# The global keys of a windowed attention: diagonal keys, and exponentials as the stationary operand

## What is computed

```
Q, K, V = x @ Wq.T + bq, x @ Wk.T + bk, x @ Wv.T + bv      # 16 heads of 8
s_loc  = Q . K over positions l-32 .. l+32, invalid ones masked
local  = softmax(s_loc) @ V_window
Kg, Vg = K[:, global_indices], V[:, global_indices]        # 25 global keys
glob   = softmax(Q . Kg * scale) @ Vg
out    = (0.7 * local + 0.3 * glob) @ Wo.T + bo
```

## Time and profile before

| | us |
|---|---|
| median of three runs | 1113.35 (1111.93 to 1116.1) |
| the profiled execution | 1111.69 |
| its span, first to last instruction | 1109.9 |
| TensorE busy | 961.9 (87%) |
| VectorE busy | 784.3 (71%) |
| GpSimd busy | 681.8 (61%) |
| ScalarE busy | 578.1 (52%) |

### The profile page before, as it was taken

How to read it: one execution, slowest core, us unless ns; L and a number is a source line. 1 busy time by engine, 2 the same in 40 slices (tenths; PEclk the granted TensorE clock), 3 DMA queues, 4 the chain that set the end, 5 groups by cost and what they waited for, 6 DMA issues and landing times.

```text
span 1109.9 us, 27990 instructions
## 1 busy us (share of the span) xinstructions
PE 961.9 (87%) x7664; PEld 709.4 (64%) x7664; DVE 784.3 (71%) x3615; ACT 578.1 (52%) x1250; POOL 681.8 (61%) x1491
## 2 busy tenths in 40 slices
PE   2999999999959995899999999999999419999950
PEld 1777777777734552677777777777776317877730
DVE  3788888888826786457776878777776327888845
ACT  2466676666621432255555555555555107777734
POOL 3566666666631222266768787888878623777765
PEclk9899999999978998599999999999999659999985
DMA  6121211111032442121112121222111157777717
GB/s 182 27 52 27 49 40 35 45 30 45 23 133 88 170 152 86 29 49 28 47 29 59 38 59 37 60 55 59 52 40 36 43 177 226 240 252 245 234 56 212
DMA packets 71376, 98.36 MB, mean 89 GB/s; under 512 B 13688, under 2 KB 43256, under 8 KB 71104
## 3 DMA queue, kind: packets, MB, share of 16 engines
q1 hardware_dynamic: 61040, 83.31, 25.6%
q0 software_dynamic: 4992, 10.30, 2.7%
q10 hardware_dynamic: 5232, 3.42, 1.2%
HBM read 49.48 MB, written 24.77 MB: 67 GB/s over the span
## 4 chain that ended last, share of the span: by engine, by line
PE 74%; DVE 9%; issue 6%; SPq 3%; DMA 3%; POOL 2%; ACT 2%; DVEq 0%; ACTq 0%; POOLq 0%
PE bank L348 6%; PE bank L172 5%; PE bank L253 4%; PE bank L357 4%; PE bank L378 4%; PE bank L1499 4%; PE bank L1500 4%; PE bank L1501 4%; PE bank L1265 4%; PE bank L412 4%; PE bank L419 3%; PE bank L168 3%; PE bank L352 3%; PE bank L387 3%; PE bank L404 2%
## 5 line engine op out<-in xcount | busy, mean ns | idle before, releaser
L536 ACT ACTIVATE p<-bank 128x480 f32<-128x480 f32 (+1 forms) x448 | 240.4, 540 | 256.3 <-PE bank L378 101.0
L671 DVE CUSTOM_DVE_ANT_0 bank<-bank,band 128x160 f32<-128x160 f32 x512 | 157.1, 348 | 80.7 <-PE bank L348 67.9
L671 DVE CUSTOM_DVE_ANT_0 bank<-bank,causal 128x128 f32<-128x128 f32 (+1 forms) x512 | 169.8, 388 | 56.4 <-PE bank L352 40.6
L901 POOL TENSOR_SCALAR_AFFINE_SELECT p<-p 128x380 f32<-128x380 f32 (+1 forms) x256 | 146.6, 602 | 63.2 <-ACT p L536 62.3
L1677 POOL DMA_INDIRECT y_rows<-p,rows x92 | 108.3, 1177 | 64.0 <-DVE p L1630 42.7
L671 DVE DVE_READ_ACCUMULATOR2_ANT nm<- 128x1 f32 x1024 | 145.5, 142 | 0.1
L882 POOL TENSOR_SCALAR_AFFINE_SELECT p<-p 128x256 f32<-128x256 f32 (+1 forms) x192 | 91.1, 486 | 69.1 <-ACT p L536 64.2
L348 PE MATMUL bank<-ks,qs 128*128 128x186 f32 x512 | 116.2, 311 | 3.1 <-issue 1.6
L348 PEld LDWEIGHTS bank<-ks,qs 128*128 128x128 f32 x512 | 79.6, 196 | 35.9 <-issue 21.0
L378 PE MATMUL bank<-qs,ks 128*128 128x160 f32 x512 | 100.4, 299 | 0.0
L1570 ACT ACTIVATE p<-bank,wb 128x512 f32<-128x512 f32 x92 | 63.6, 691 | 39.4 <-PE bank L1501 24.3
(11 more groups left out here) (209 smaller groups left out, 2369.0 us busy)
## 6 DMA issues: line engine op xcount, KB each, us to landing
qs<-parts SPq DMA_DIRECT2D x46, 512.0 KB
qs<-qf SPq DMA_DIRECT2D x128, 128.0 KB, 2.4
rows<-xr SPq DMA_DIRECT2D x23, 260.0 KB
parts<-ks SPq DMA_DIRECT2D x8, 512.0 KB
xs<-x_b SPq DMA_DIRECT2D x16, 256.0 KB
p<-in_w SPq DMA_DIRECT2D x12, 256.0 KB
xin<-in_x SPq DMA_DIRECT2D x16, 128.0 KB, 2.2
parts<-qf SPq DMA_DIRECT2D x4, 512.0 KB
```

Of the source, the lines that this page charges most:

```text
L536: act.activation(pb[:, :, :].rearrange("p u c -> p (u c)")[:, lo:lo + cols], bank[:, 0:cols], ACT.Exp, scale=SCALE).then_inc(L.exp_done, 1)
L671: return dve.tensor_tensor_reduce(at, at, mask, -1.0, -BIG, ALU.add, ALU.min, nm[:, item:item + 1])
L901: pool.affine_select(out=at, in_=at, compare_op=ALU.is_ge, fill=0.0, base=base, pattern=[[0, 4], [sign, hi - lo]], channel_multiplier=-sig ...
```

## The change

For the global keys of the second attention:

- `T.kg` becomes 128 columns wide for each t, with the keys of head group j in rows 32j and columns 32j of a block diagonal. One product of this with all 128 rows of the queries gives the scores of four heads, so pass 2 has its unit u = 3 only in j = 2 and 3, with two products of 256 columns each, in fp32r. They take the queries of all j from `T.qf`, of which there are now three, and which gets the rows of the maxima by four more transfers on SP's queue. `keep_kg` writes the diagonal with four `tensor_scalar` of 32 rows instead of one of 128, after pass 2 of (3,3), and counts `kg_kept` twice, once after the two copies and once at the end.
- ScalarE has two exponentials of 512 columns into `T.pg` instead of four of 256. Part 2 of `pv` is gone. In its place `global_values`, in (0,0) of the next iteration behind `round_pj(0)`, has the exponentials as the stationary operand and 64 columns of `vgb` moving, eight products, and leaves queries by channels in `T.og`. So `round_og` and the copy to `ogs` are gone, and `mx0` now stands behind `pj0` in its bank.
- `keep_vg` has one instruction instead of four.
- `round_kg` moves ahead, into (3,3) behind pass 1, and `keep_kg` behind the maxima of (3,3), ahead of `chosen` and `both_choices`. The identity products are gone.
- The new buffers lie in the room where the last layer holds its rows. Semaphore values are adapted; `unit2` numbers the units of pass 2. GpSimd clears the wider `kg` once at the start.

```
+        return 3 + 14 * (i - 1) + (0, 3, 6, 10)[j] + (u if j < 3 or i < B else u - 3)
...
+        if local and u == 3:
+            return self.late and j > 1
+        return self.pass2[j] and u < 3
...
-ROUNDS = (("pj0", "og", "mx0", "ont", "mx1", "y", "q1", "xt", "mx3"),
+ROUNDS = (("pj0", "mx0", "ont", "mx1", "y", "q1", "xt", "mx3"),
...
-        def round_og():
-            bank_read("og", i, p, th)
-            pe.wait_ge(L.ov_kept, L.kept * fin + 2)
+        def global_values():
+
+            pe.wait_ge(L.exp_done, L.unit2(i - 1, 3, 3) + 1)
+            pe.wait_ge(L.vg_kept, fin + 1)
+            wait(pe, L.on_done, fin)
             for tau in range(2):
-                for r in range(2):
-                    m = turn(T.mi[0][:, (2 * tau + r) * P:(2 * tau + r + 1) * P],
-                             T.ogs[:, r, tau * P:(tau + 1) * P])
-            m.then_inc(L.ot_done, 1)
+                out = T.og[:, tau * S:(tau + 1) * S].rearrange("p (r t z) -> p r t z", r=2, t=4)
+                for t in range(4):
+                    m = pe.matmul(out[:, :, t, :], T.pg[t // 2][:, t % 2 * S + tau * P:t % 2 * S + (tau + 1) * P],
+                                  T.vgb[p][:, t, :].rearrange("p (r z) -> p r z", r=2),
+                                  start=tau == 0 and t == 0, stop=True, skip_group_check=True)
+            m.then_inc(L.pg_done, 1)
...
-        def keep_array_busy():
-
-            wait(pe, L.red_done, L.units * (4 * i + 3) + 3)
-            for _ in range(4):
-                pe.matmul(T.s1[0][:, 0:P], T.ident[:], T.ident[:], start=True, stop=True)
...
+                    pe.wait_ge(L.kg_kept, 2 * i + 1)
...
             if L.local and u == 3:
-                for t in range(4):
-                    m = pe.matmul(bank[32 * t:32 * t + 32, 0:S], T.kg[par][:, t, :], q[:, t, :].bitcast(F32),
-                                  start=True, stop=True)
+                pe.wait_ge(L.kg_kept, 2 * i)
+                for c in range(2):
+                    t = 2 * (j - 2) + c
+                    m = pe.matmul(bank[:, c * S:(c + 1) * S], T.kg[n][:, t, :], T.qf[(i - 1) % 3][:, t, :],
+                                  start=c == 0, stop=True, skip_group_check=True)
...
-            if part == 2:
-                if j == 0:
-                    pe.wait_ge(L.vg_kept, i)
-                pe.wait_ge(L.exp_done, 4 * step + 4)
-                m = pe.matmul(T.og[:, r * S:(r + 1) * S], T.vgb[n][:, j, :], pb[:, 3, 0:S],
-                              start=j == 0, stop=False, skip_group_check=True)
-            elif L.local:
+            if L.local:
...
-                if j == 0 and u == 2 and th.finish and L.local:
-                    round_og()
+                if j == 0 and u == 0 and th.finish and L.local:
+                    global_values()
...
+                if L.local and (j, u) == (3, 3) and th.prep:
+                    round_kg()
                 if u == L.units - 1 and th.max_step(j) and not (L.local and j == 0):
                     round_mx(j)
-                if th.pass2[j]:
+                if th.pass2_unit(L.local, j, u):
                     pass2(j, u)
-                if th.late and u > 0:
+                if th.late and u in (1, 2):
...
-        if L.local and th.prep:
-            round_kg()
-            keep_array_busy()
...
-                act.copy(T.ogs[:, :, :], T.og[:, :].rearrange("p (r q) -> p r q", r=2)).then_inc(L.ov_kept, 1)
...
+            if L.local and u == 3:
+                wait(act, L.pg_done, i - 1)
+                act.activation(T.pg[j - 2], bank[:, :], ACT.Exp, scale=SCALE).then_inc(L.exp_done, 1)
+                return
...
-            for s in range(2):
-                for r in range(2):
-                    m = dve.tensor_tensor(out[:, r, s, :, s, 0:DH], vg[:, r, s, :, :], mask, ALU.mult)
-            m.then_inc(L.vg_kept, 1)
+            wait(dve, L.pg_done, i - 1)
+            vg = T.mi[1][:, 0:D].rearrange("p (t j d) -> p t j d", t=4, j=4)
+            out = T.vgb[p][:, :, :].rearrange("p t (j c) -> p t j c", j=4)
+            mask = T.diag[:, :].rearrange("p (o j d) -> p o j d", o=1, j=4).to_broadcast([P, 4, 4, DH])
+            dve.tensor_tensor(out[:, :, :, 0:DH], vg, mask, ALU.mult).then_inc(L.vg_kept, 1)
...
-                dve.tensor_copy(T.ks[n][:, :, lo:lo + NGE], kg[:, :, 0:NGE])
-            dve.tensor_scalar(T.kg[n][:, :, 0:NG], kg[:, :, 0:NG], T.rows[:, 0:1], None,
-                              ALU.add).then_inc(L.kg_kept, 1)
...
+                m = dve.tensor_copy(T.ks[n][:, :, lo:lo + NGE], kg[:, :, 0:NGE])
+            m.then_inc(L.kg_kept, 1)
+            if i > 0:
+                dve.wait_ge(L.p2_done, L.unit2(i, 3, 3) + 1)
+            for j in range(4):
+                own = slice(32 * j, 32 * j + 32)
+                m = dve.tensor_scalar(T.kg[n][own, :, 32 * j:32 * j + NG], kg[own, :, 0:NG], T.rows[own, 0:1], None, ALU.add)
...
+            m.then_inc(L.kg_kept, 1)
...
+                if L.local and (j, u) == (3, 3) and th.prep:
+                    keep_kg()
...
+                if L.local:
+                    qf = T.qf[(i - 1 if j == 0 else i) % 3]
+                    sp.dma_start(qf[32 * js + 24:32 * js + 24 + L.parts, :, :].bitcast(F32),
+                                 T.mt[js][0:4 * L.parts, :].bitcast(F32)).then_inc(L.mrow[js], 16)
...
+        T.qf = [qf[:, :, :], part_of(0, S), part_of(4 * S, S)]
+        T.kg = [part_of(8 * S, P), part_of(8 * S + 4 * P, P)]
+        T.pg = [T.p[k][:, 3, :] for k in range(2)]
```

More of the change, by code:

```diff
@@ L53, in __init__ @@
         self.parts = 4 if local else 2
-        self.kept = 2 if local else 1
+        self.rows_sent = 32 if local else 16
         def s(what):
@@ L91, in __init__, with unit2 @@
             self.steps = 22
+    def unit2(self, i, j, u):
+        if not self.local:
+            return 3 * (4 * i + j - 3) + u
+        if i == 0:
+            return u
+        return 3 + 14 * (i - 1) + (0, 3, 6, 10)[j] + (u if j < 3 or i < B else u - 3)
 class There:
@@ L174, in in_iteration @@
     def in_iteration(name, i, p, th):
-        if name in ("og", "vg", "kg", "rt", "rl", "rp") and not L.local:
+        if name in ("vg", "kg", "rt", "rl", "rp") and not L.local:
             return False
@@ L209, in bank_read @@
             "k1": (L.k_kept, 2 * k + 4), "xt": (L.xt_kept, k + 3),
-            "vg": (L.vg_kept if L.local else None, k + 1), "kg": (L.kg_kept if L.local else None, k + 2)}[last]
+            "vg": (L.vg_kept if L.local else None, k + 1), "kg": (L.kg_kept if L.local else None, 2 * k + 4)}[last]
         wait(pe, signal, value)
@@ L338, in pass1 @@
                 if L.local:
-                    pe.wait_ge(L.kg_kept, i + 1)
+                    pe.wait_ge(L.kg_kept, 2 * i + 1)
             if u == 0:
@@ L363, in pass2 @@
             par, batch = (n, i - 1) if j < 3 else (p, i)
-            unit = L.units * (4 * i + j - 3) + u
-            bank = T.s2[u % 2 if L.local else (j + u) % 2]
+            unit = L.unit2(i, j, u)
+            bank = T.s2[unit % 2 if L.local else (j + u) % 2]
             if u == 0:
-                pe.wait_ge(L.mrow[js], L.q_base + 16 * batch + 16)
+                pe.wait_ge(L.mrow[js], L.q_base + L.rows_sent * (batch + 1))
             wait_apart(pe, L.passed, L.exp_done, unit - L.ring2 + 1)
@@ L497, in keep_mx @@
             act.wait_ge(L.mx_done, 4 * i + j)
-            wait(act, L.mrow[js], L.q_base + 16 * batch)
+            wait(act, L.mrow[js], L.q_base + L.rows_sent * batch)
             rows = 4 * L.parts
@@ L529, in exp @@
             pb = T.p[(j + 1) % 2]
-            bank = T.s2[u % 2 if L.local else (j + u) % 2]
-            cols = (S if u == 3 else len(local_items(u)) * WIN) if L.local else 512
-            act.wait_ge(L.p2_done, L.units * step + u + 1)
+            unit = L.unit2(i, j, u)
+            bank = T.s2[unit % 2 if L.local else (j + u) % 2]
+            act.wait_ge(L.p2_done, unit + 1)
+            if L.local and u == 3:
+                wait(act, L.pg_done, i - 1)
+                act.activation(T.pg[j - 2], bank[:, :], ACT.Exp, scale=SCALE).then_inc(L.exp_done, 1)
+                return
+            cols = len(local_items(u)) * WIN if L.local else 512
             if u == 0:
                 wait(act, L.pv_done, step - 1)
-            lo = 3 * WIN * u if L.local and u < 3 else 512 * u
+            lo = 3 * WIN * u if L.local else 512 * u
             act.activation(pb[:, :, :].rearrange("p u c -> p (u c)")[:, lo:lo + cols], bank[:, 0:cols], ACT.Exp,
@@ L818, in body @@
                     layernorm()
-        if L.local and th.prep:
-            keep_kg()
     iterations(dve, L.local, body)
```

71 lines of the change are left out of this document (36 added, 35 removed).

## The result

The changed kernel takes 1204.33 us (median of four runs, 1183.95 to 1223.21) against 1113.61 for the kernel before on the same chip. By the medians it is 8.1% slower, where 1.2% faster was forecast; the ratio of the comparable executions is 1.072, 95% interval 1.066 to 1.079.

What follows compares the result with a forecast made beforehand. TensorE was taken to set the pace in the second attention. Savings in most batches, less new waits in odd ones (+3.6 us), summed to -13.5 us: 1098.2 profiled, 1100 us median, 1.2% less; range 1080 to 1118.

Steps and rivals of the forecast that it cites:

- granted clock 1.00 from the second batch on: Sign expected in the profile after: TensorE keeps its full clock, 1.00, from the second batch on.
- (b): Rival: clock falls at the six `rp` waits, low for 7 or 10 us of work; 1114 or 1123 us; chance 0.20.
- 0.96 us, they hide a wait: Identity products at the batch's end: removal saves 0.96 us; they hide pass 1 (0,0)'s wait for VectorE's two key copies.
- `global_values`: Added TensorE work in (0,0): eight products, 16 records at 0.109 us, 1.74 us a batch; ends 1.4 and 2.0.
- Segment A: From pass 1 (3,3) to the next batch's pass 1 (0,0): 2.1 us instead of 3.39, including a 0.25 us wait.
- Segment B: From pass 1 (0,0) to pass 1 (1,1): 8.4 us instead of 7.36, with a 1.1 us wait at pass 1 (1,1).
- Segment C: The rest of the batch, from pass 1 (1,1) to pass 1 (3,3): 1.5 us less.
- A plain batch: A whole batch without added `rp` or GpSimd waits: -1.3 + 1.0 - 1.5 = -1.8 us.
- The wait at `rp`: Start of odd batches 5 to 15: TensorE newly waits 2.2 us (1.5 to 2.6) for VectorE, six times.
- GpSimd: Odd batches, masks of j = 2: TensorE waits about 0.4 us (0 to 0.6) for their first half, half counted.
- Rival (a): VectorE waits stay small, so TensorE's own sum holds: -2.9 us a batch, 1068 us; chance 0.22.
- (c): Rival: `qf` row transfers come late for diagonal units in pass 2; 0.5 us at two units a batch, 1115 us; chance 0.08.

Runs made afterwards that it cites:

- e2: The kernel before with only its identity products taken out; 1132.8 us, ratio 1.015 to 1.025 to the kernel before.
- e7: The changed kernel with `round_kg`, `keep_kg` and identity products in their old places, so only diagonal keys and stationary exponentials remain; 1172.3 us.
- e11: e5 plus three products of 512 columns ahead of pass 1 (j,3) in each j; 1131.0 us.
- e3: The changed kernel with `round_rp` moved behind `global_values` in (0,0); 1176.5 us.
- e10: e3 with GpSimd's bias addition moved from j = 2 to j = 0; 1144.1 us.
- e15: e10 plus the four identity products of 128 columns at the batch border; 1124.9 us.
- e12: e6 with GpSimd's bias addition moved from j = 2 to j = 0; 1117.1 us.
- e5: The changed kernel with `round_rp` behind `global_values` and four border products of 512 columns in one pass; 1152.9 us.
- e8: The kernel before with only the global keys picked and copied in (3,3) and no identity products; 1103.8 us, ratio 0.992 to 0.998.
- e6: e5 plus five products of 512 columns ahead of pass 1 (1,0), filling the wait for `normalise`; 1144.8 us.

## Why the prediction was wrong, step by step

**The step that failed** is "granted clock 1.00 from the second batch on". I had a rival for it, (b), at a chance of 0.20, and priced it at the six waits for `rp` alone with 7 or 10 us of low clock each, 14 to 23 us. In place of this the clock falls fourteen times in the second attention. Six of the falls are at the borders with `rp`, as rival (b) had it, but they last 116 us together instead of 42 or 60; the other eight, 143 us, are at places that it didn't count, down to a border with waits of no more than 0.34 us. So rival (b) was right in kind, right in six places, and too small by a factor of four to seven (14 to 23 us priced over the forecast of 1100, 104 measured). Two steps led there. I costed the identity products as a cover for one wait only, "0.96 us, they hide a wait", though e2 shows that the kernel before needs them for its clock. And I counted the removed products as time alone: what parts 1 and 2 remove is 256-column work next to the lightest places of the batch, and what they add in one of those places is sixteen records of 64 columns. e7 shows that these parts bring the loss; that it is through this exchange of dense for light work is argued from the rows, not shown by a run.

**Where the time went**: the stage is 107 us longer. Its early batches at the full clock save time (23.4 us against 24.3), so the low clock can account for the loss: 260 us at half the clock cost up to 130, less the waits that are swallowed in them. Restoring the streams (e11) brings the clock to 1.00 from 500 to 850 us, and removing or filling waits one after another (e3, e10, e15, e12) brings the time from 1204 to 1117 without restoring the streams in each j. That both help is shown. What exactly tips the clock at one border and not at the next is not: the borders at 498.94 and 545.78 have the same rows. In e15, with its border filled, it falls at 502 us behind the wait for `normalise`, and in the changed kernel it holds behind the same wait at 508.96. The Trainium skill (TensorE: Matmul & The Clock Gate, "A second HAM failure mode: psum-queue depth-cycling") tells of a kernel in which short idles of TensorE between groups of products make the clock oscillate; the windows at 547 and 548, busy 0.63 and then 0.88 with the clock going from 1.00 to 0.58, agree in kind.

**The terms of the sum**, read in the batches at the full clock:

- `global_values`: 1.74 us forecast, 1.70 measured. The price by the stationary block held.
- Segment A: 2.1 forecast, 1.86 measured in the early batches, with a wait of 0.15 us where 0.25 was forecast. In the late odd batches this term failed: pass 1 (0,0) waits 2.4 to 2.6 us five times, since VectorE isn't through with the maxima of (3,3) when the sum takes it to be. The working counts the routing on VectorE, but not the layer norm beside GpSimd's masks.
- Segment B: 8.4 forecast, 9.51 measured. `normalise` does come back as a wait, but at `round_pj(1)`, which stands behind `ot` in its bank, and not at pass 1 (1,1). So 1.40 us of waiting instead of 1.1, with the 1.05 us of `pj1` and a part of pass 2 behind the wait instead of ahead of it. I also missed that `round_pj(0)` now stands behind ScalarE's copy of `mx3`, 0.34 us.
- Segment C: 1.5 us less forecast. The batch is 23.42 us, so C is 23.42 - 1.86 - 9.51 = 12.05; before it was 24.27 (global keys at 496.48 and 520.75) - 3.39 - 7.36 = 13.52. So 1.47 us less: right.
- A plain batch: 1.8 us less forecast, 0.85 measured, the difference being B.
- The wait at `rp`: 2.2 us forecast, 1.3 to 1.65 measured, six times, 9.3 us together. Right in place; at five of the six the wait of segment A comes on top.
- GpSimd: I looked for a wait for the masks, 0.4 us. The one that came was for the bias behind the masks, up to 1.97 us in e5. "The masks of j = 2" was the right stretch and the wrong instruction. In the changed kernel TensorE waits for it once between 500 and 960 us, 1.02 us at 603.92.

**Rival (a)** fell with B and with the clock, and **(c)** didn't occur: nowhere among the waits from 500 to 960 us does pass 2 wait for the rows of `qf`.

Even with the clock held, parts 1 and 2 add nothing to part 3 in an early batch. An early batch takes 23.4 us in e8 (part 3), in e7 (parts 1 and 2: 23.38, global keys at 488.10 and 511.48), in the changed kernel and in e12 (all three). TensorE is busy 23.11 us in e8 and 21.39 in the changed kernel: the 1.7 us that parts 1 and 2 take off it are waited away for `normalise` (1.40), ScalarE (0.34) and the copies (0.15). The gains don't add up, since behind TensorE's own work the chain from the maxima of (0,2) over `normalise` to `pj1` is next.

The best version that these runs point to is e8, 1103.8 us, faster than before by 0.5% (0.2 to 0.8). It isn't known whether part 1 or part 2 weighs more; no kernel had one without the other.

## What to carry to other kernels

Ahead of removing cheap or dummy products from a TensorE-bound loop, list the places where light products and waits stand together, and ask for each what dense work is left beside it; a fall of the clock there cost 8 us a batch here, nine times what the edit saved. Test it by removing the filler alone in the old kernel (e2) before the big change: that one line would have shown 2% lost through the clock, though not the size of the whole. And look at what else runs on the engine that a moved wait depends on: here a copy moved ahead came behind a layer norm slowed beside the masks. A chain that waits just behind the bound, here maxima, `normalise`, `pj1`, caps what several savings give together.

## What the runs showed of the hardware

- The width of the filling products made no difference to the time: 128 columns in two passes or 512 in one gave 1153.2 and 1152.9, and 1124.9 and 1124.3 us.
- Two normalising instructions of VectorE took 1.87 us beside GpSimd's masks (711.11 in the changed kernel, above) and 1.89 us in e6 (617.30), where pass 1 (0,0) waited 1.64 us for what was queued behind them. Without the masks beside them two such instructions take 0.60 us (at 874.83 us in e8). The Trainium skill (GPSIMD Engine Reference, "Key points") says that GpSimd shares its SBUF interfaces with VectorE, with contention for certain VectorE instructions, those in a two-port mode or with two SBUF inputs. The rows agree in kind; whether these instructions are of that sort no run shows, and no run took the masks away.
